# Second mixture's routed tiles: inner rows copied by VectorE, staged weights by ScalarE

## The reference

```
def _swiglu(x, wa, wb, wo):
    return jax.nn.silu(x @ wa.T) * (x @ wb.T) @ wo.T
...
for i in range(N_ROUTED):
    y = y + _swiglu(xf, w1[i], w3[i], w2[i]) * combine[:, i:i + 1]
z = _swiglu(xf, sw1, sw3, sw2)
return (y + z).reshape(shape)
```

## Time and profile before

| | us |
|---|---|
| median of 3 runs | 383.82 (381.99 to 384.12) |
| the profiled execution | 383.59 |
| its span, first to last instruction | 381.8 |
| routed loop of the second mixture, first to last result copied to `y_sb` | 296.5 to 364.9 |
| first mixture, gate and up products | 55.5 to 221.6 |

### The profile page before, as it was taken

How to read it: one execution, slowest core, us unless ns; L and a number is a source line. 1 busy time by engine, 2 the same in 40 slices (tenths; PEclk the granted TensorE clock), 3 DMA queues, 4 the chain that set the end, 5 groups by cost and what they waited for, 6 DMA issues and landing times.

```text
span 381.8 us, 6944 instructions
## 1 busy us (share of the span) xinstructions
PE 325.0 (85%) x2160; PEld 184.3 (48%) x2160; DVE 207.4 (54%) x639; ACT 151.2 (40%) x322; POOL 118.1 (31%) x118
## 2 busy tenths in 40 slices
PE   8966588999999999999999978059838998989991
PEld 6635454555555655555555544047413444444440
DVE  2778875445655454555555422863953545455337
ACT  1655321333333444333344433273511444455531
POOL 0022051212522224322112211321663665664320
PEclk9985558999999999999999996555956999999996
DMA  7999939994311172222118892320021232222136
GB/s 245 331 291 281 301 74 322 305 268 101 55 30 29 27 205 32 40 38 33 14 15 239 258 303 33 110 82 29 0 52 47 76 89 73 91 77 70 42 136 222
DMA packets 21145, 48.39 MB, mean 127 GB/s; under 512 B 2600, under 2 KB 11688, under 8 KB 20088
## 3 DMA queue, kind: packets, MB, share of 16 engines
q1 hardware_dynamic: 14680, 35.78, 30.4%
q0 software_dynamic: 6048, 11.28, 13.9%
q10 hardware_dynamic: 384, 0.90, 0.7%
HBM read 37.98 MB, written 9.96 MB: 126 GB/s over the span
## 4 chain that ended last, share of the span: by engine, by line
PE 72%; DVE 9%; DMA 7%; issue 4%; ACT 4%; POOL 2%; SPq 1%; DVEq 0%; ACTq 0%; POOLq 0%
PE bank L1349 26%; PE bank L1323 22%; PE bank L1389 9%; PE bank L1313 5%; PE bank L1167 4%; PE bank L1175 2%; PE bank L1227 2%; DMA rows<-rows 2%; DMA wgu<-results 2%; DVE st L737 2%; DMA sums<-y_sb,route_dst 1%; DVE z L815 1%; ACT rows L514 1%; DMA rows<-sums 1%; DMA x_in<-rows,route_tok 1%
## 5 line engine op out<-in xcount | busy, mean ns | idle before, releaser
L1349 PE MATMUL bank<-wgu,xT 128*64 x320 | 99.4, 465 | 1.5 <-DVE xT L1010 0.9
L1349 PE MATMUL bank<-rows,xT 128*64 128x344 f32 x320 | 99.4, 465 | 0.0
L1323 PE MATMUL bank<-wdn,hT 120*64 (+2 forms) x396 | 90.8, 392 | 8.9 <-ACT hT L589 7.3
L1323 PEld LDWEIGHTS bank<-wdn,hT 120*64 120x64 f32 (+1 forms) x396 | 49.1, 140 | 49.1 <-issue 23.4
L412 POOL DMA_INDIRECT sums<-y_sb,route_dst x20 | 31.6, 1580 | 118.6 <-ACT y_sb L625 86.7
L1349 PEld LDWEIGHTS bank<-wgu,xT 128*64 128x64 f32 x320 | 43.0, 139 | 47.6 <-issue 8.2
L1323 PE MATMUL bank<-rows,hT 120*64 120x256 f32 x240 | 56.8, 388 | 0.0
L404 POOL DMA_INDIRECT x_in<-rows,route_tok x43 | 43.1, 1003 | 37.4 <-PE bank L1167 13.9
L990 DVE SCALAR_TENSOR_TENSOR hh<-th,bank 128x344 f32<-128x344 f32 x40 | 20.5, 513 | 58.9 <-ACT th L578 58.9
L1349 PEld LDWEIGHTS bank<-rows,xT 128*64 128x64 f32 x320 | 43.0, 139 | 0.0
L578 ACT ACTIVATE th<-bank 128x344 f32<-128x344 f32 x40 | 18.3, 457 | 60.6 <-PE bank L1349 60.6
(11 more groups left out here) (154 smaller groups left out, 455.5 us busy)
## 6 DMA issues: line engine op xcount, KB each, us to landing
wgu<-gu SPq DMA_DIRECT2D x8, 1376.0 KB, 17.7
wdn<-wd SPq DMA_DIRECT2D x8, 720.0 KB, 22.4
wgu<-gu SPq DMA_DIRECT2D x3, 1408.0 KB, 6.7
wdn<-wd SPq DMA_DIRECT2D x5, 576.0 KB, 8.7
rows<-rows SPq DMA_DIRECT2D x8, 256.0 KB, 4.2
wgu<-results SPq DMA_DIRECT2D x4, 512.0 KB, 5.7
wgu<-gu SPq DMA_DIRECT2D x1, 1056.0 KB, 5.5
rows<-xt SPq DMA_DIRECT2D x4, 256.0 KB, 7.9
```

Source lines behind the costliest of these rows:

```text
L1323: last = mm(psum[7][part, 0:H], hT[0:m.wide, j * P:(j + 1) * P][:, part], wd(j), start=(j == 0), stop=(j == m.chunks - 1))
L1349: last = mm(psum[2 * c + g][part, 0:CH0], xT[:, r, k * P:(k + 1) * P][:, part], w, start=(k == 0), stop=(k == KH - 1))
```

## The change

In the routed part of the second mixture, two jobs change places. The copy of the turned inner rows from bank 4 to `hT` goes from ScalarE to VectorE (new `copy_hT1`, a tensor_scalar by 0.5, first in VectorE's step). The copy of gate and up weights to `stage_gu1` goes from VectorE to ScalarE (`stage_gate_up1`, with its read of the expert's number), which then makes both staged copies. TensorE waits for `hT_copied_v` in these 27 steps. The four shared tiles ahead of the loop keep ScalarE's copy.

```diff
@@ scalar
-            def copy_hT(m, s, r):
+            def copy_hT(m, s):
...
+            def stage_gate_up1(t):
+
+                expert = second_owner(m1, t)
+                nc.scalar.activation(stage_gu1[:, t % 2, :], wgu[:, bass.ds(expert * GU1 + GU1, GU1)],
+                                     ACT.Copy).then_inc(m1.gu_staged, 1)
+
...
+            stage_gate_up1(0)
+            stage_gate_up1(1)
             stage_down1(0)
             stage_down1(1)
             tanh_half(m1, NS, 0)
+            stage_gate_up1(2)
             tanh_half(m1, NS + 1, 1)
+            stage_gate_up1(3)

             def step1(s, r):
-                copy_hT(m1, s + NS, r)
                 if s < LATE - 2:
                     tanh_half(m1, s + (NS + 2), r % 2)
+                if s < m1.S - 4:
+                    stage_gate_up1(s + 4)
                 if s < m1.S:
                     act.wait_ge(m1.y_done, s + (NS + 1))
@@ vector
+            def copy_hT1(s):
+
+                dve.wait_ge(m1.hT_done, s + NS + 1)
+                nc.vector.tensor_scalar(hT[0:m1.wide, 0:NF1 * P], psum[4][0:m1.wide, 0:NF1 * P], 0.5, None,
+                                        ALU.mult).then_inc(m1.hT_copied_v, 1)
...
-            dve.wait_ge(m1.experts_ready, 1)
-            for n, (_, gu_a, gu_z, dn_a, dn_z) in enumerate(second_weights()):
-                dve.wait_ge(w1_here[n], 16 * (gu_z > gu_a) + 16 * (dn_z > dn_a))
-            stage_gate_up1(0)
-            stage_gate_up1(1)
             copy_xT(m1, 0, 0)
             copy_xT(m1, 1, 1)
             dve.wait_ge(m1.h_made, NS)
             hidden(m1, NS, 0, m1.half)
-            stage_gate_up1(2)
             copy_xT(m1, 2, 0)
             hidden(m1, NS + 1, 1, m1.half)
-            stage_gate_up1(3)

             def step1(s, r):
+                copy_hT1(s)
                 if s < m1.S - 3:
                     copy_xT(m1, s + 3, (r + 1) % 2)
                 if s < LATE - 2:
                     hidden(m1, s + (NS + 2), r % 2, m1.half)
-                if s < m1.S - 4:
-                    stage_gate_up1(s + 4)
@@ tensor
             def down(m, s, first, second):
-                pe.wait_ge(m.hT_copied_a, s + 1)
+                if m.n == 0 or s < NS:
+                    pe.wait_ge(m.hT_copied_a, s + 1)
                 if m.n == 0:
                     pe.wait_ge(m.hT_copied_v, s + 1)
+                elif s >= NS:
+                    pe.wait_ge(m.hT_copied_v, s + 1 - NS)
```

More of the change, by code:

```diff
@@ L617, in step0 @@
             def step0(s, r):
-                copy_hT(m, s, r)
+                copy_hT(m, s)
                 if s < m.S - 1:
@@ L677, in _ @@
             for i in range(NS):
-                copy_hT(m1, i, i % 2)
+                copy_hT(m1, i)
                 if i + 2 < NS:
@@ L1022, in stage_gate_up0 @@
                                           ).then_inc(mix[0].gu_staged, 1)
[L1024 to L1028, removed]
             m = mix[0]
```

## The result

The changed kernel is slower, not faster. Its median is 390.5 us (four runs, 385.7 to 390.8) against 383.5 us of the kernel before, a ratio of 1.018 with a 95% interval of 1.014 to 1.023. Forecast were 376.7 us and a range up to 381.0. The profiled execution took 390.4 us, with a span of 388.6. Times in us are from here on medians of all runs of a kernel, while ratios leave out the runs more than 1.5% above the kernel's fastest, so that where a kernel's times spread wide its ratio can be about 1% under that of the medians.

What follows compares the result with a forecast made beforehand. The prediction took a closed ring through ScalarE, with TensorE inside it, to bound the kernel. Loop -7.4, ahead of it -1.1 and behind it +1.6 took 383.6 to 376.7 us, range 374.2 to 381.0.

Steps and rivals of the forecast that it cites:

- The ring: In the loop, result copy, staging, inner-row copy and down product wait in a circle, 2.92 us a period; cutting it gives -7.4.
- the estimate of 0.88: ScalarE's new weight copy in the loop by the skill's rule, in us; the prediction itself used 0.79.
- For which TensorE waits only a whole step later: In the loop, a late result message delays only the result copy, which TensorE needs a whole step later.
- Done at 3.08, the next turn ends at 3.20. No cost.: In VectorE's queue, inner rows of tile s+2 end before the next turn does, so they don't delay the `hT` copy.
- a slack of 0.7 for news of a turn: In the loop, VectorE's copy to `hT` ends near 0.9 and is wanted at 1.55, leaving about 0.7 us.
- The lateness: While gathers run, TensorE's result messages come some 0.75 us late, about one in every two steps.
- Late messages still count in part: Rival, chance 0.14: in the loop VectorE's in-order queue passes lateness on, 4.8 us come back, 381.0, or 378.9 if half.
- Array late: Rival, chance 0.07: TensorE's array itself loses 0.65 us in every unbroken gathering step of the loop, giving 386.0.
- ScalarE's ring: Rival, chance 0.05: slow register reads make ScalarE's own load the loop's period, 3.02 us, adding 4.6 and giving 381.3.
- Full clock later: Rival, chance 0.10: at the entry, TensorE's earlier products run at 1.2 GHz for longer, costing 1.8 and giving 378.3.
- -1.1 for the entry: Ahead of the loop, an earlier `xT` copy starts TensorE 1.4 us earlier; taken as -1.1 for the clock, between -2 and +0.5.
- The end: Behind the loop, VectorE adds and combines only after the last inner-row copies: 1.8 later, less a 0.23 wait, +1.6 us.

Runs made afterwards that it cites:

- the kernel with the result first: Changed kernel with ScalarE's result copy moved ahead of the gate and up staging: 381.4 us, ratio 0.989 to the kernel before.
- the fifth group: Kernel before at 382.5 us; reordered kernel with the down product one step later 379.3 us, 0.989; changed kernel with only the result copy first 381.9 us, 0.996.
- The first group: Kernel before at 383.1 us; rows-only half 1.006, weights-only half 0.995, changed kernel with result copy first 0.989, or with expert's number read ahead of the wait 0.996.
- the early read: Changed kernel in which TensorE reads the expert's number ahead of its wait for the result copy: 382.7 us, ratio 0.996 to the kernel before.
- the half change: Kernel before with only the inner-row copy to `hT` moved to VectorE, gate and up weights still staged by VectorE: 384.9 us, ratio 1.006.
- the third group: Its run meant here: changed kernel, result copy first, inner rows later, expert's number read early, last two `hT` copies on ScalarE: 0.989, against 0.983 without these two.
- the rows behind: Changed kernel with one edit, VectorE making a tile's inner rows one step later, behind the copy to `hT`: ratio 0.992 to the kernel before.

## Why the prediction was wrong

**The ring**: right. Without late messages the kernel before runs at 2.93 a step (64.5 over 22) and the changed one at TensorE's pace, 61.6 where 60.5 was worked out. ScalarE's new copy is 0.79, as said, and its load never bound: the kernel with the result first has the same load and 0.989, or 0.996 in the fifth group. (The Trainium skill, "ScalarE: Activation LUTs", in its rules for kernel authors, budgets 0.3 us for an ACTIVATE whose bias is a pointer operand, and this copy has none. So the estimate of 0.88 that the prediction took from it is not for this copy: the row has 0.79.)

**"For which TensorE waits only a whole step later"**: this is the step that failed first. The prediction put the result copy behind tanh and the new staging and took it for free. But there is one bank for results, so the copy of tile s stands between TensorE and the down product of tile s+1, in the very next step, and the slack there was about 0.1 us, not a step. On time it doesn't show. With late news the chain is tanh, staging, copy, read of the expert's number: 0.65, 0.69, 0.37 and 0.9 us. In the kernel before the staging was not there, and the read lay beside the wait for `hT`. The first group shows both terms by taking each away: no wait of 2 us with the result first, and 0.15 for 0.9 with the early read.

**"Done at 3.08, the next turn ends at 3.20. No cost."**: no cost on time, but also no slack: 0.12 us. The text spoke of a slack of 0.7 for news of a turn, and gave late news of a gate product only a remark and 0.5 us for the whole loop. In the changed order such news goes through tanh and inner rows to the next `hT`; the half change and the kernel with the result first show it, with waits of 2.18 and 0.89 us.

**The lateness was taken as fixed.** It was read as 0.75 and about one in two steps. The count held. The size did not: in the changed kernel it is 1.3 to 2.2 us. The row that pointed there was in the text (tanh at 334.92 for rows done at 333.26, 1.6 late) and was used only to prove that the array was not late. A sum with 2 us at one step in two would have given seven waits of up to 2 us; six came, of 9.6 us in all.

**The rivals.** "Late messages still count in part" had the right cause, but named VectorE's queue, where in the changed kernel ScalarE's result copy ended last (at 321.92, the copy to `hT` at 321.60), and priced it at 4.8 us of the gain where the loss is 13.3 (74.9 - 61.6). "Array late" gave 386.0, the nearest figure, and its mechanism is refuted: TensorE's next product is on time each time, and without gathers unheld steps cost 2.78. ScalarE's ring: refuted. Full clock later: it came. The first product starts 2.78 earlier, of which 1.45 lie ahead of the change's place and 1.3 are its gain, but the first result copy is only 1.1 earlier, so 1.7 went back, near that rival's price of 1.8. The forecast's -1.1 for the entry thus came out by luck. What no rival had is the clock in the loop: behind two of the six waits the granted clock is 0.50 for 3.4 us, 1.7 us of work each. (The Trainium skill, "TensorE: Matmul & The Clock Gate", Part 1, has throttling as the default that activity releases; the trace agrees, with 0.50 granted behind the wait that ended at 307.79.)

**The end**: +1.4 for +1.6, right in size. That it could be won back by leaving two copies on ScalarE was an expectation of the third group, and wrong: the results' way through memory was next.

**The range**: its lower end, 374.2, counts the entry twice. It takes 2.0 for an early clock off a forecast that already holds 1.1 of it; 376.7 - 0.5 - 0.9 is 375.3. The measured time lies off the other end, so this didn't decide.

**Which chip**: the loss of 1.8% was measured where messages are late. On another such chip it was 0.1% by the ratio (0.996 to 1.006) and 1.2% by the medians, so even there its size is not settled. No unchanged run of the changed kernel was made on the quiet chip; near it stand 0.990 without gathers and 0.992 with the rows behind.

## What to carry to other kernels

Before a ring is cut, write down for every wait of the bound engine how late its releaser's own news may be until it counts, the slack, and take the smallest; a queue that is idle half the time can have a slack of 0.1 us. Where one buffer (here PSUM bank 7) is handed back by a copy, nothing goes ahead of that copy in its queue. And when edits that differ give the same good result, look whether the kernel before changed too: here it was the chip.

## What was new about the hardware

Messages of TensorE came up to 2.6 us late (tanh at 308.14 for a product that ended at 305.48), in bunches (four of them within 0.2 us), at most about once in two steps, while the products behind them ran on time. All eleven traces from chips where the kernel before takes 382 to 384 us, and with gathers, have them. None is in three traces without gathers, of which one, from such a chip, tells something; and none in six traces with gathers on the one chip where the kernel before takes 377.5 us, the only quiet chip met. The bunches were let go 0.3 to 1.1 us after a gather's issue ended (gather 306.19 to 307.16, news 308.14; gather 318.46 to 319.43, news 320.2), but gathers held nothing up on the quiet chip. What holds the messages, why every second step, and why the lateness grows when TensorE runs unheld, stays open. One more thing goes with it: in each of the eleven traces with late messages, 2 to 17 of the some 60 message records of TensorE between 295 and 345 us are missing, and in the nine without, none is. So that the recording itself takes part can't be excluded by these runs.

TensorE's granted clock fell to 0.50 inside the loop behind some waits of 1.4 to 2.2 us, in four traces (both of the changed kernel, the half with rows only, the early read), not behind all such waits, and in no loop whose waits stayed at 1.1 us or under.
